# Softmax attention in a four-layer block: first value products ahead of V's projection, and V's copy behind the third exponential

## The reference, cut to what matters

```python
x = x + _layernorm(_L1_attn_ref(_layernorm(x), gamma, beta, w_qkv, w_out))

def _L1_attn_ref(x, ln_gamma, ln_beta, w_qkv, w_out):    # 16 heads of 64
    xn = layernorm(x) * ln_gamma + ln_beta
    q, k, v = split(xn @ w_qkv, 3)                       # to heads
    q = concat([q[head 0], rope(q[heads 1:])])           # by position, k too
    dots = einsum('bhqd,bhkd->bhqk', q, k) * SCALE
    attn = softmax(dots)
    out = einsum('bhqk,bhkd->bhqd', attn, v)
    return out.reshape(B, N, 1024) @ w_out
```

## Time and profile before

| | |
|---|---|
| median of three runs | 1271.09 us |
| profiled execution, own time | 1273.35 us |
| its span, first to last instruction | 1271.5 us |
| TensorE matmul busy, weight load busy | 1152.8 us (91%), 941.7 us (74%) |
| VectorE, ScalarE, GpSimd busy | 986.7 (78%), 771.9 (61%), 568.4 us (45%) |
| mean granted TensorE clock | 0.976 |
| first and last scores of the attention stage | 457.9 and 1045.8 us |

### The profile page before, as it was taken

The page is one execution under the profiler, slowest core; times in us unless marked ns, Lnnn a source line. Parts: engine busy times, 40 slices in busy tenths (PEclk is TensorE's granted clock), DMA queues, the critical chain, the costliest instruction groups (busy, mean ns, idle before and its releaser), DMA issues.

```text
span 1271.5 us, 32080 instructions
## 1 busy us (share of the span) xinstructions
PE 1152.8 (91%) x10554; PEld 941.7 (74%) x10554; DVE 986.7 (78%) x2499; ACT 771.9 (61%) x2314; POOL 568.4 (45%) x729
## 2 busy tenths in 40 slices
PE   3888886789898869999999999999999997999997
PEld 3555554688888747777777777777777766999997
DVE  6688885588888777778788778787877876788885
ACT  2445553222222249888989888899888894344342
POOL 2777775444444554444545445445444342011112
PEclk9999998799999989999999999999999998999999
DMA  8000000000000000000000000000000000000000
GB/s 282 10 2 0 0 1 2 1 2 1 0 1 0 1 1 2 1 2 1 2 2 1 0 0 0 0 0 0 0 0 0 2 1 1 6 13 12 8 12 19
DMA packets 14303, 12.32 MB, mean 10 GB/s; under 512 B 1778, under 2 KB 12564, under 8 KB 13972
## 3 DMA queue, kind: packets, MB, share of 16 engines
q1 hardware_dynamic: 14228, 11.34, 2.9%
HBM read 9.24 MB, written 2.10 MB: 9 GB/s over the span
## 4 chain that ended last, share of the span: by engine, by line
PE 56%; DVE 14%; issue 8%; POOL 4%; ACT 1%; DVEq 1%; POOLq 0%; ACTq 0%
PE bank L191 14%; PE bank L976 10%; PE bank L1041 10%; PE bank L1070 10%; PE bank L1083 5%; PE bank L840 4%; POOL rstd L365 2%; DVE stat L298 2%; DVE hT L1230 1%; DVE gg L1222 1%; PE bank L795 1%; DVE yn L314 1%; POOL X L370 1%; DVE mv L303 1%; DVE fh_hi L1191 1%
## 5 line engine op out<-in xcount | busy, mean ns | idle before, releaser
L993 ACT ACTIVATE work<-bank,work 128x256 f32<-128x256 f32 x512 | 236.0, 474 | 60.0 <-DVE work L985 59.2
L985 DVE TENSOR_REDUCE work<-bank 128x2 f32<-128x512 f32 x256 | 164.0, 682 | 113.2 <-PE bank L976 113.2
L1007 POOL TENSOR_TENSOR work<-work 128x512 f32<-128x512 f32 x64 | 66.7, 1041 | 279.0 <-DVE work L1001 279.0
L959 POOL TENSOR_TENSOR work<-work 128x512 f32<-128x512 f32 x128 | 164.3, 1284 | 30.2 <-DVE work L951 15.8
L1013 ACT ACTIVATE work<-work 128x256 f32<-128x256 f32 x384 | 161.7, 509 | 0.0
L1041 PE MATMUL bank<-ident,work 128*128 128x128 f32 x1024 | 141.9, 279 | 5.1 <-DVE work L949 1.6
L1041 PEld LDWEIGHTS bank<-ident,work 128*128 128x128 f32 x1024 | 111.7, 141 | 38.5 <-issue 19.9
L1070 PE MATMUL bank<-work 128*64 128x256 f32 x1024 | 138.5, 392 | 0.5 <-DVE work L1056 0.5
L840 PE MATMUL bank<-WrT,moe_work 128*128 128x128 f32 x1024 | 137.4, 278 | 0.7 <-POOL moe_work L817 0.7
L363 POOL TENSOR_SCALAR ve<-mv 128x2 f32<-128x2 f32 x128 | 28.6, 223 | 240.1 <-DVE mv L303 240.1
L976 PE MATMUL bank<-work 32*128 32x256 f32 x2048 | 130.4, 391 | 2.6 <-ACT work L993 1.6
(11 more groups left out here) (176 smaller groups left out, 2903.9 us busy)
## 6 DMA issues: line engine op xcount, KB each, us to landing
X<-in_x SPq DMA_DIRECT2D x4, 512.0 KB, 5.9
wF<-in_L_ffn_h_w SPq DMA_DIRECT2D x2, 1024.0 KB, 9.7
out<-X SPq DMA_DIRECT2D x16, 128.0 KB, 1.8
w_qkv<-in_L_attn_w_qkv SPq DMA_DIRECT2D x1, 1536.0 KB, 9.2
WrT<-in_L_ffn_Wr SPq DMA_DIRECT2D x1, 1024.0 KB, 5.1
w_out<-in_L_attn_w_out SPq DMA_DIRECT2D x1, 512.0 KB, 10.5
wF<-in_L_ffn_w_w SPq DMA_DIRECT2D x2, 256.0 KB, 8.5
rope_sin<-in_rope_sin SPq DMA_DIRECT2D x1, 256.0 KB, 3.2
```

The costliest lines, as they stand in the source:

```text
L959: nc.gpsimd.tensor_tensor((QT if kind == "q" else KT)[:, p, a, :], rc[:, ru % 2, :], rs_[:, ru % 2, :], ALU.add).then_inc(c_rope, 1)
L985: nc.vector.tensor_reduce(nmax[:, QUAD * a + j, :], SB_[j][:, :].rearrange("p (t k) -> p t k", t=T), AX.X, ALU.max, negate=True).then_inc( ...
L993: ins = nc.scalar.activation(pr[:, a % 2, j, t, :], SB_[j][:, t * LEN:(t + 1) * LEN], ACT.Exp, bias=nmax[:, h, t:t + 1], accum_out=psum_[: ...
```

## The change

Two moves; no instruction is added or removed. On ScalarE the copy of V for the next sequence is issued behind the exponentials of head 2 instead of behind those of head 1. On TensorE the value products of heads 0 and 1 of the slot before are issued in front of V's unit instead of behind it. The slot's other order stays.

```diff
@@ scalar, sa_step @@
                     for j in range(QUAD):
                         sa_exp_scalar(act, i, a, j)
-                        if j == 1 and not i_is(i, SEQS - 1):
+                        if j == 2 and not i_is(i, SEQS - 1):
                             sa_v_scalar(act, i + 1, 1 - p, a, UB_["v"])
                     sa_norm_scalar(act, i, a, 1)
@@ tensor, sa_step @@
                     if i_is(i, 0) and a == 0:
                         pe.wait_ge(d_ternary, 1)
+                    if last:
+                        sa_pv_tensor(pe, *last, 0)
                     if more:
                         pe.wait_ge(c_pta, reached(2 * n))
                         sa_unit_tensor(pe, i + 1, 1 - p, a, "v", UB_["v"])
-                    if last:
-                        sa_pv_tensor(pe, *last, 0)
-                    if more:
                         pe.wait_ge(c_ptv, reached(2 * (n - 1) + 1))
                         sa_unit_tensor(pe, i + 1, 1 - p, a, "q", UB_["q"])
                         pe.wait_ge(c_ptv, reached(2 * (n - 1) + 2))
```

## The result

The changed kernel took 1290.74 us (median of four runs, 1287.04 to 1293.09) against 1271.43 of the kernel before; the ratio is 1.0148, 95% interval 1.0122 to 1.0174. So it is slower by 15.5 to 22 us; the medians lie 19.3 apart. In two kernels of the experiments one execution took far longer than all the others (1621 and 2208 us), and it is left out of their medians and ratios. Forecast were 1287.2 us and 16.1 us slower, range 1280.5 to 1293.

What follows compares the result with a forecast made beforehand. The prediction took ScalarE's chain behind head 2's maximum, ending in head 1's turn, as the bound. Its terms 6.6 + 1.4 + 5.6 + 2.5 = 16.1 us on 1271.1 gave 1287.2 us (74%), range 1280.5 to 1293.

Steps and rivals of the forecast that it cites:

- Head 2's exponential doesn't move: ScalarE, normal slots: it waits for its maximum, so still starts 5.2 us after the scores, ScalarE idle about 0.45 ahead.
- V's copy costs 0.47: ScalarE: behind head 2's exponentials nothing covers the copy, so all behind it moves by 0.47 us (0.39 to 0.57).
- Slot 0 and sequence 0: Full 0.47 us per slot: 6.6 in slot 0, sequences 1 to 14; 1.4 in slots 1 to 3, sequence 0.
- Slot 3: Sequences 1 to 14: head 1's turn has some 0.07 us of slack, so each loses 0.40, together 5.6.
- Slots 1 and 2: Sequences 1 to 14: the late output copy delays the next scores, 0.09 us in each of 28 slots, 2.5 together.
- The total: Whole kernel: the slots' losses sum to 16.1 us slower, 1271.1 + 16.1 = 1287.2 us.
- TensorE's part: Value products ahead of V's unit: 0 us; saved changes gain nothing, some 0.1 lost for bank 0 is covered.
- R1: TensorE bounds and V's copy held head 2's exponential: faster or not slower, 1264 to 1271, about 1269 us; 6%.
- R2: ScalarE's idle time is moved, not added, and every slot keeps its length: no change, 1271 us; 2%.
- R3: Only slots that now wait visibly (slot 0, and sequence 0) lose: 8.0 us, 1279 us; 10%.
- R4: Value products' wait for bank 0 or later handings over add 6 to 8 us from sequence 1 on: 1294 us; 6%.
- R5: Longer stalls let TensorE's granted clock fall to 0.95 over 560 us, adding 28 us: 1315 us; 2%.

## Why the prediction was right

**Head 2's exponential doesn't move.** Right: 5.22 against 5.21 us, and the wait of 0.45 that it forecast at about 0.45. That V's copy had lain in this wait was shown twice: by taking the wait away, and by shortening the copy, each in both places.

**V's copy costs 0.47.** Right: 812.80 to 813.28 is 0.48. The row that gave it was the one slot of the stage in which VectorE has no copies to make. The covered distance, 0.57, would have been the wrong one: it ends with a wait and not with the copy.

**Slot 0 and sequence 0.** 6.8 and 1.5 against 6.6 and 1.4.

**Slot 3.** 6.0 against 5.6: the term was mis-sized. I took 0.07 of slack off each, because the eight loads seemed unbroken. They are not. Head 1's first load, in a window of its own in the trace before:

```profile
831.22 0.14 PEld L1041 LDWEIGHTS bank<-ident,work 128*128 128x128 f32 x1
```

This load starts 0.12 behind the normalization's end and 0.19 behind the load ahead of it, where the others lie up to 0.11 apart. TensorE was already waiting in the loop's slots 3, and there was no slack to take off. (The 0.05 of handing over that I used is that of the unrolled slots; in the loop it is 0.12.) The ten in the hardware loop lose 0.48 in the even sequences, and 0.32 to 0.42 in the odd ones, behind which the loop turns. The four outside the loop lose 0.44 to 0.49. That the loop's turn would simply move along was wrong in part: it takes in 0.06 to 0.16 of the delay. Why was not tried.

**Slots 1 and 2.** 2.9 against 2.5, practically all of it inside the loop, and unevenly: slot 1 loses 0.15 to 0.16 or 0.24 to 0.28 in turns, slot 2 loses 0.07 to 0.08, and the unrolled slots lose nothing (up to 0.01). I had 0.09 for each of the 28, so that this sum came near is in part luck. The step was right (the output copy is late), as the kernel with this copy early showed.

**The total.** The slots lost 17.2 us against 16.1. The medians differ by 19.3; the remaining 2.1 us are not in the stage's trace, and the interval of 15.5 to 22 takes them in.

**TensorE's part.** 0 was right, but one piece of the reasoning was not. No 0.1 is lost for bank 0: the value products start 2.96 us into the slot in slot 0, and the same where bank 0 is empty a whole microsecond earlier (in slot 2 it is empty at 1.33, in slot 0 at 2.61). What eats the saved changes is the distance from the turns to them, 0.18 more than the turns had to V's unit (2.96 against 2.78 from 797.03 less 794.25); so what is saved is given back, and the second value products stand still at 6.29.

**The rivals.** R1 and R2 fell by the rows of slot 0, R3 by slots 1 to 3, R4 by the sum of 17.2, and R5 by the clock, which stayed at 1.00, 2.4 GHz, in this window with TensorE's matmuls busy for 77.89 of 80 us where they had been 79.51. Behind sequence 0 the clock fell inside the stage in one trace alone, that of TensorE's order by itself, once, at a cost of 1.6 us. The occupancy of ScalarE in the same window fell, from 70.26 to 68.47, as the kernel got slower: it measures work, not what is waited for.

```profile
700.00:780.00 80.00, 77.89 (x734) 59.77 (x728) 62.16 (x123) 68.47 (x219) 37.93 (x42) 1.00 0.00 0
```

## What to carry to other kernels

An instruction on a busy engine can be free in one place and cost its whole length one place later: look for the wait that it lies in, by asking whether the instruction behind it starts at its end or at a fixed distance from another engine's result. The true price of such an instruction is read where its cover is missing, in a first or last iteration. And when two places both cost, look at the order of the engine that is waited for; here one line on VectorE undid all of the loss, and on top of it a reciprocal issued earlier and a normalization taken off the chain gave more.

## What the runs showed of the hardware that I had not expected

Handing over from one engine to another takes longer at some places of the hardware loop than at the same places of the unrolled code, and not at all of them. The times are from the producer's end to the consumer's start, in the trace after:

| from, to | unrolled | loop |
|---|---|---|
| maximum, exponential of head 0, slots 0 and 1 | 0.03 | 0.12 to 0.13 |
| the same, slots 2 and 3 | 0.03 | 0.03 |
| normalization, turn of head 1, slots 0 and 3 | 0.05 | 0.12 to 0.13 |
| output copy, next scores, slot 2 | | 0.13 |
| output copy, next scores, slot 1 | | 0.13 in odd, 0.22 to 0.26 in even sequences |

The unrolled slots 1 and 2 have the copy end at 10.11 us and the next scores start at 10.16 to 10.17. That is the length that they had before, so it is not shown that TensorE waits for the copy there. In the loop the value that is waited for depends on the loop's counter; but that is so in slots 2 and 3 too, where ScalarE's wait is as short as outside. What makes the difference stays open.
